# Score matmuls on half the rows of the array, and three buffers that are no longer cleared

## What is computed

```python
query = qt_c + qt_r                                   # 4 batches, 16 heads, 512 x 8
key = kt_c + kt_r
attn = jnp.einsum('bhqd,bhkd->bhqk', query, key) / scale   # scale = 12
attn = jax.nn.softmax(attn, axis=-1)
out = jnp.einsum('bhqk,bhkd->bhqd', attn, value)
```

## Time and profile before

| | us |
|---|---|
| median of 3 runs | 472.19 |
| lowest, highest | 470.93, 472.37 |
| profiled execution, span from first to last instruction | 471.8 |

### The profile page before, as it was taken

One profiled execution on the slowest core, in us unless ns is written; L12 is line 12 of the kernel. 1 busy time (PEld: TensorE's weight loads), 2 busy tenths in 40 slices (PEclk: granted clock), 3 DMA queues, 4 the chain that ended last, 5 costly groups with the idle time before them and its releaser, 6 DMA issues.

```text
span 471.8 us, 6744 instructions
## 1 busy us (share of the span) xinstructions
PE 357.8 (76%) x1871; PEld 154.1 (33%) x1871; DVE 291.1 (62%) x569; ACT 203.0 (43%) x377; POOL 170.0 (36%) x191
## 2 busy tenths in 40 slices
PE   5589667899999999999999989531154989872750
PEld 3343201223333323333233444330033556550530
DVE  5998998877777787787777571467871233221120
ACT  2323330777777777777777655010011233221110
POOL 2835751151111110011111271200026588887673
PEclk9999955899999999999999999955557899897695
DMA  8202466222222111111111150000322356554331
GB/s 243 51 0 67 158 231 214 69 69 68 70 67 66 60 56 62 58 56 58 63 64 34 34 158 2 22 1 0 109 84 84 88 116 137 109 111 73 45 28 17
DMA packets 37794, 36.58 MB, mean 78 GB/s; under 512 B 5648, under 2 KB 28944, under 8 KB 37776
## 3 DMA queue, kind: packets, MB, share of 16 engines
q1 hardware_dynamic: 31632, 29.94, 20.4%
q0 software_dynamic: 6144, 6.43, 8.4%
HBM read 24.56 MB, written 11.60 MB: 77 GB/s over the span
## 4 chain that ended last, share of the span: by engine, by line
PE 50%; POOL 16%; DVE 13%; issue 11%; SPq 3%; DMA 3%; ACT 2%; another core or an unknown queue 1%; DVEq 0%; ACTq 0%; POOLq 0%
PE ps L1140 14%; PE ps L1154 14%; PE ps L1121 10%; POOL out L497 7%; POOL ex L486 3%; DVE big L904 3%; DVE mx L790 2%; PE ps L1326 2%; PE ps L1358 2%; SPq L273 2%; PE ps L1165 2%; SPq L282 2%; DMA ex<-rows,idx 1%; PE ps L1205 1%; POOL big L392 1%
## 5 line engine op out<-in xcount | busy, mean ns | idle before, releaser
L790 DVE TENSOR_REDUCE mx<-ps 128x2 f32<-128x1024 f32 x128 | 151.6, 1220 | 37.8 <-PE ps L1121 37.6
L602 ACT ACTIVATE big<-ps 128x512 f32<-128x512 f32 x256 | 145.2, 597 | 59.6 <-PE ps L1140 58.1
L1140 PE MATMUL ps<-EQ,EK 128*128 128x512 bf16 x256 | 95.3, 388 | 5.4 <-ACT big L602 1.7
L1121 PE MATMUL ps<-MK,MQ 128*128 128x512 bf16 x256 | 83.3, 411 | 7.6 <-DVE mx L790 4.6
L1154 PE MATMUL ps<-big,VA 128*32 128x512 f32 x512 | 68.2, 604 | 1.6 <-ACT osb L579 1.1
L1140 PEld LDWEIGHTS ps<-EQ,EK 128*128 128x128 bf16 x256 | 24.6, 97 | 105.4 <-ACT big L602 94.4
L497 POOL DMA_INDIRECT out<-big,idx x32 | 50.5, 1579 | 14.3 <-issue 8.8
L486 POOL DMA_INDIRECT ex<-rows,idx x32 | 34.1, 1065 | 57.7 <-DVE idx L1013 43.1
L648 ACT ACTIVATE big<-ps,b1c 128x512 f32<-128x512 f32 x32 | 22.0, 688 | 63.7 <-PE ps L1326 58.8
L1326 PE MATMUL ps<-big,w1s 128*128 128x512 f32 x64 | 36.3, 688 | 2.8 <-ACT big L648 1.7
L416 POOL COPY VA<-Vall 128x128 f32 (+1 forms) x16 | 4.6, 290 | 86.8 <-PE ps L1154 86.8
(11 more groups left out here) (165 smaller groups left out, 414.2 us busy)
## 6 DMA issues: line engine op xcount, KB each, us to landing
MK<-k_parts SPq DMA_DIRECT2D x32, 96.0 KB
MQ<-q_parts SPq DMA_DIRECT2D x32, 96.0 KB
EK<-k_parts SPq DMA_DIRECT2D x32, 96.0 KB
EQ<-q_parts SPq DMA_DIRECT2D x32, 96.0 KB
w1s<-in_w SPq DMA_DIRECT2D x8, 256.0 KB
w2s<-in_w SPq DMA_DIRECT2D x8, 256.0 KB
k_parts<-big SPq DMA_DIRECT2D x4, 384.0 KB, 3.2
q_parts<-big SPq DMA_DIRECT2D x4, 384.0 KB, 3.7
```

The costliest lines, as they stand in the source:

```text
L602: nc.scalar.activation(PT[:, u, 2 * i + half, kc, :], ps[:, 4 + half, :], ACT.Exp, scale=SCALE).then_inc(s_ex, 1)
L790: nc.vector.tensor_reduce(mx[:, u, :].rearrange("p (h a) -> p h a", h=2)[:, :, n], ps[:, 2 * (n % 2):2 * (n % 2) + 2, :], AX.X, ALU.max, n ...
L1121: ins = mm(ps[:, 2 * (n % 2) + half, :], MQ[:, u, i, qc * 128:(qc + 1) * 128], MK[:, u, half, i, :], start=True, stop=True)
L1140: mm(ps[:, 4 + half, :], EK[:, u, i, kc * 128:(kc + 1) * 128], EQ[:, u, half, i, :], start=True, stop=True).then_inc(s_sc, 1)
```

## The change

MK and EQ lose their plane per half: both halves lie in one buffer, on their own partitions, as in MQ and EK. Each matmul of `max_unit` and `exp_unit` takes only its half's partitions, 48 or 51 from partition 0 or 64. Nothing reads the zeros then, so MQ, MK and EQ are not cleared, and SyncE waits for one memset (EK's ones). MK's memory is half as large; h2T gets a buffer of its own. The order of instructions on every engine is unchanged, the three memsets aside.

```diff
-        MQ, EK = (sb(n, [128, 2, 2, L], bf16) for n in ("MQ", "EK"))
-        MK, EQ = (sb(n, [128, 2, 2, 2, L], bf16) for n in ("MK", "EQ"))
+        MQ, EK, MK, EQ = (sb(n, [128, 2, 2, L], bf16) for n in ("MQ", "EK", "MK", "EQ"))
...
-        mk_place = flat(MK, "abct").bitcast(fp32)
-        xn2 = mk_place[:, 0:2 * L].rearrange("p (u c d) -> p u c d", u=2, c=TC)
-        h2T = mk_place[:, 2 * L:4 * L].rearrange("p (u t) -> p u t", t=L)
+        xn2 = flat(MK, "abt").bitcast(fp32).rearrange("p (u c d) -> p u c d", u=2, c=TC)
+        h2T = sb("h2T", [D, 2, L])
...
-                        sp.dma_start(buf[rows, slot, half] if buf in (MK, EQ) else buf[rows, slot],
-                                     src.rearrange("o j d i t -> (o j) d (i t)")).then_inc(done, 16)
+                        sp.dma_start(buf[rows, slot], src.rearrange("o j d i t -> (o j) d (i t)")).then_inc(done, 16)
...
-                        sp.dma_start(EQ[r:r + 1, slot, half].rearrange("p i q -> p (i q)"),
+                        sp.dma_start(EQ[r:r + 1, slot].rearrange("p i q -> p (i q)"),
...
-            sp.wait_ge(s_one, 4)
+            sp.wait_ge(s_one, 1)
...
-            for buf in (MQ, MK, EQ):
-                nc.gpsimd.memset(buf[:], 0.0).then_inc(s_one, 1)
...
-                    ins = mm(ps[:, 2 * (n % 2) + half, :], MQ[:, u, i, qc * 128:(qc + 1) * 128], MK[:, u, half, i, :],
-                             start=True, stop=True)
+                    rows = slice(64 * half, 64 * half + PR)
+                    ins = mm(ps[:, 2 * (n % 2) + half, :], MQ[rows, u, i, qc * 128:(qc + 1) * 128],
+                             MK[rows, u, i, :], start=True, stop=True)
...
-                mm(ps[:, 4 + half, :], EK[:, u, i, kc * 128:(kc + 1) * 128], EQ[:, u, half, i, :],
+                rows = slice(64 * half, 64 * half + PR + 3)
+                mm(ps[:, 4 + half, :], EK[rows, u, i, kc * 128:(kc + 1) * 128], EQ[rows, u, i, :],
                    start=True, stop=True).then_inc(s_sc, 1)
```

## The result

The changed kernel takes 467.63 us (median of 4 executions, 464.96 to 467.82), the kernel before, run beside it on the same chip, 472.00 (470.93 to 472.37). The ratio is 0.9887, 95% interval 0.9857 to 0.9918 (the quotient of the two medians is 0.9907, inside the interval): 4.4 us faster where 11 were forecast, and 0.1 above the top of the range. The profiled execution has a span of 465.9 and a time of 467.69, so 1.8 us lie around the span.

A forecast was written before the change was run, and what follows sets the result against it. TensorE was full but ACT's exponentials gated the loop, and SyncE's DMA queue covered 52.04 to 94.59 us. Terms −6.5 − 5.5 + 0.5 = −11.5 took 472.2 to 460.7, said as 461; range 455.5 to 467.5.

The forecast's parts named there:

- Memsets, −6.5: Preparation: without three POOL memsets VectorE runs on sooner, the first MK load and all behind it come 6.5 us earlier.
- Two of L683 slip in: Preparation, better case: two of VectorE's last four L683 run between the first two remaining memsets; the rest ends at 18.4.
- The pairs: Attention loop: the two half-row matmuls of a max_unit overlap, taking 0.22 us instead of 0.43.
- regular stretch: Loop, one exp matmul behind a weigh block to the next: 3.05 us falls to 2.90, two such per step.
- The loop, −5.5: Steps 1 to 13: 3.9 us saved in regular stretches, 1.3 with max_turn, 0.3 with out_turn.
- The change of height: Loop, around out_turn: switching the array between half and full height costs 0.1 us each way.
- the stretch with out_turn: Loop: the pair gives 0.21 us, height changes eat 0.2, so the stretch is near 3.45.
- The free case, 455: Rival for the loop: changing the array's height costs nothing, time 455 us; chance 0.14 (454 to 458).
- Steps 14 and 15, +0.5: Last steps, without pairs: overlapping exps gain 0.2 us about eight times, some 22 height changes cost 0.1 each: net +0.5.
- the clock, the other side: Rival before the loop: less TensorE work, clock rises late, 464 us (chance 0.08), or stays low, 528 (0.05).
- the first stretches cost 1.3 more each: Loop's start, late-clock rival: each first stretch takes 1.3 us more, time 464; chance 0.08.
- Span to time, 0.4: Whole kernel: profiled span 471.8 against median time 472.2 us, so 0.4 lies around the span.

The follow-up runs named there:

- e4: Kernel before, with the clearing of MQ, MK and EQ moved from POOL to ACT: 467.91 us against 475.16 for the kernel before (0.9849).
- e10: Changed kernel plus unread full-height matmuls in both maxima rounds, around step 1's max_turn and in step 0: 467.28 us against 474.43 before (0.9847).
- e7: Changed kernel with half rows for the maxima only; exps on all rows, EQ's planes cleared by ACT: 464.48 us against 471.67 before (0.9854).
- e8: Changed kernel with half rows for the exps only; maxima on full rows, MQ and MK cleared by ACT: 481.82 us against 471.67 before (1.0214).
- e12: As e10 (changed kernel plus extra full-height matmuls), but none of them in step 0: 470.56 us against 474.43 before (0.9908).
- e11: As e10 (changed kernel plus extra matmuls), but the extra ones take 64 rows instead of 128: 479.25 us against 474.43 before (1.0105).
- e3: Changed kernel with the memsets of MQ, MK and EQ put back on POOL: 472.88 us against 475.16 before (0.9945).

## Why the prediction was wrong

The step that failed is the clock: the prediction took it that a step 0 of half-height matmuls without gaps would raise it as before. Second to it, the loop's term was mis-sized.

- *Memsets, −6.5:* right. The first MK load moved by 6.66, step 1 by 6.70. The agreement to 0.2 is partly luck: L702 ends 7.4 earlier (18.75 against 26.12) where 6.9 was taken, and VectorE's wait for the value matmuls grew by 0.7 where 0.4 was taken. That VectorE is what waits, not POOL, is shown by e4: the same clearing on ACT gives back the same time. "Two of L683 slip in", the better case, is what happened.
- *The pairs:* right. A pair occupies 0.22 or less between neighbours, and the regular stretch is 2.87 (2.90 said). The second exp even follows the first by 0.23 where 0.45 was said, which brings nothing, as ACT is not ready for it. The Trainium skill (TensorEngine Tiling, Theoretical Speedup) gives up to 2× for a contraction of 64 or less; the trace agrees for the pair (0.43 to 0.22 or less). Of the 1.7 us of array time that eight pairs save, a step keeps 0.33.
- *The loop, −5.5:* too large, about −4.0 (0.33 for each of eleven steps, 0.35 from max_turn to the first out_turn in e10, and the end of the loop). Two of four stretches were taken as regular; in one of them ACT copies mxn, which was not in the working. Steps −0.33, not −0.42.
- *The change of height:* right in size. 0.1 into full height, 0.1 to 0.15 out; the stretch with out_turn is 3.51 (near 3.45 said). By the Trainium skill (TensorEngine Tiling, Key Properties) a change of tiling mode drains the engine; e7 and e8 agree, with 0.1 each way where the cost had been put. The free case, 455, has fallen.
- *Steps 14 and 15, +0.5:* 0.9 by the trace, and 1.6 more in executions in which the clock dips in step 15.
- *The clock:* here it failed. The text had the mechanism as a rival, "the clock, the other side", and gave it 0.08 at 464. Its price was off: "the first stretches cost 1.3 more each" is near (4.3 against 2.9), but there are up to five of them, 2.6 to 7.0 us. And the argument against it was wrong. "In step 0 at the low clock a turn still has 0.43 + 0.86 = 1.29 of matmul against some 1.2 of VectorE" is what the trace shows: turns start 1.29 apart (83.49, 84.78, 86.08) and the busy share is near full. From this the text concluded that the clock would rise. The result and e10 to e12 show that it does not follow: half-height matmuls fill the busy share and the clock stays at 0.50, to 110 us in the changed kernel. The earlier trace rows had been read as "busy, so it rises", with a kernel in which busy and full height were the same thing.
- *Span to time, 0.4:* 1.8 in these runs, so the execution profiled before had a time near 473.6, 1.4 above the median shown, and was none of the timed ones (470.93 to 472.37). The forecast was a difference taken off the median, and the size of the difference was not touched by it.

In sum: −11.5 forecast; the loop is 1.5 smaller, the end 0.4 larger, the clock takes 2.6 to 7.0, which gives −7 to −2.6, and the runs have −4.4, −6.1 and −4.6. Why the clock rises when it does, at 97, 102 and 110 us in three executions of the same kernel, is open: until then the only full-height work in step 1 is the weigh blocks and the transposes, and no experiment varied those.

## What to carry over

Before cutting what a matmul occupies of the array, look where the clock rises and which matmuls TensorE runs just there: a busy share in the profile does not say that they raise it, and it pays to keep them at full height until it is up. A clearing on an engine that holds another one up can be moved, not only removed; here moving it gave all of the head's gain, and more than the change as made. In a loop where ACT releases two exps of a stretch, count ACT's own extra work in each of its stretches before multiplying one stretch's gain by all.

## What the hardware showed that was not expected

- Matmuls on 48, 51 or 64 rows kept TensorE at 4.00 of 4 us busy in the records at a granted clock of 0.50 (e11, windows from 56 to 100 us); matmuls of 128 rows in the places of the extra ones had it at 1.00 from 57 us on (e10). With the clock up, half-height matmuls without weigh blocks lost it within step 0 (e12, 81 us); with weigh blocks between them, as in the loop, it stays at 1.00. Full-height maxima between half-height exps had TensorE at 4.00 of 4 us and the clock at 0.50 from 80 to 92 us (e8).
- VectorE gets in between some memsets that follow one another and not between others. In e3 an operation of L680 that began at 15.25 took 3.54, through the memset of EK and that of MQ behind it; the ones after it got in at 18.8, where MQ's ended and MK's had begun.
- The experts' stage, with its indirect DMAs, takes 108.5 to 109.4 us on two of the chips and 111.4 to 112.7 on two others (each measured on one occasion), and for the changed kernel's and the earlier kernel's versions alike.
